# Tokenizer of a vision tower: GpSimd's first chunk products wait for VectorE's coefficients

## The reference

```
dt = exp(log_dt)
dt_Lambda = dt * Lambda                      # complex, [128 heads, 64 states]
S = exp(dt_Lambda[..., None] * t - P_max)    # t = 0..511
num = exp(dt_Lambda_neg) - 1
den = exp(dt_Lambda_neg * L) - 1
x = den * Lam
Wc = W * num * conj(x) / (x * conj(x) + 1e-7)
K = einsum('chn,hnl->chl', Wc, S).real       # [16, 128, 512]
h = concat([cls_tok, K])                     # the tokens of all later layers
```

## Time and profile before

| | |
|---|---|
| median of 3 runs | 1603.04 us (1602.81 to 1603.46) |
| the profiled execution's own time | 1603.07 us |
| its span, first to last instruction | 1601.3 us |
| TensorE busy | 1392.8 us (87%) |
| VectorE busy | 844.9 us (53%) |
| ScalarE busy | 373.8 us (23%) |
| GpSimd busy | 480.3 us (30%) |
| mean granted TensorE clock | 0.964 |

### The profile page before, as it was taken

One profiled execution on the slowest core, in us unless ns is written; L12 is line 12 of the kernel. 1 busy time (PEld: TensorE's weight loads), 2 busy tenths in 40 slices (PEclk: granted clock), 3 DMA queues, 4 the chain that ended last, 5 costly groups with the idle time before them and its releaser, 6 DMA issues.

```text
span 1601.3 us, 20910 instructions
## 1 busy us (share of the span) xinstructions
PE 1392.8 (87%) x6461; PEld 1080.7 (67%) x6462; DVE 844.9 (53%) x1711; ACT 373.8 (23%) x711; POOL 480.3 (30%) x350
## 2 busy tenths in 40 slices
PE   0295667999899999379999899999999989899996
PEld 0293325888544444136777588888888879888895
DVE  8895488655322222464667775555555533333332
ACT  1022213211111111142223312333233212122221
POOL 0480620152144443100111025523333111333442
PEclk9999788999999999789999999999999999999998
DMA  4294003301765554600000303666656578666543
GB/s 97 53 165 65 0 0 131 127 21 42 280 161 94 95 96 76 197 26 0 1 0 1 140 20 122 195 219 211 223 202 208 215 301 294 181 182 182 95 85 40
DMA packets 87386, 193.95 MB, mean 121 GB/s; under 512 B 28657, under 2 KB 32753, under 8 KB 83825
## 3 DMA queue, kind: packets, MB, share of 16 engines
q1 hardware_dynamic: 67232, 151.18, 29.2%
q0 software_dynamic: 20096, 42.02, 14.2%
HBM read 112.24 MB, written 77.87 MB: 119 GB/s over the span
## 4 chain that ended last, share of the span: by engine, by line
PE 74%; DVE 12%; DMA 9%; issue 2%; ACT 1%; POOL 0%; SPq 0%; POOLq 0%; DVEq 0%; ACTq 0%
PE ps L1505 21%; PE ps L1565 19%; PE ps L1626 9%; PE ps L2027 6%; PE ps L1652 4%; PE ps L427 4%; DMA out<-held,moe_scratch 3%; PE ps L1599 2%; DVE held L480 2%; DMA held<-xn_rows,moe_scratch 2%; DMA out<-moe_scratch 2%; PE ps L536 1%; PE ps L776 1%; PE ps L777 1%; PE ps L1640 1%
## 5 line engine op out<-in xcount | busy, mean ns | idle before, releaser
L1565 PE MATMUL ps<-moe_rounded 128*128 128x384 f32 (+2 forms) x1800 | 374.9, 350 | 0.0
L1565 PEld LDWEIGHTS ps<-moe_rounded 128*128 128x128 f32 x1800 | 326.3, 188 | 33.2
L1275 DVE SCALAR_TENSOR_TENSOR held<-ps,moe_scratch,held 128x512 f32<-128x512 f32 (+1 forms) x255 | 187.5, 748 | 180.1 <-PE ps L1505 180.0
L1505 PE MATMUL ps<-moe_expert_parts,moe_rows_parts 128*128 (+1 forms) x1320 | 260.1, 350 | 4.7 <-DVE moe_rows_parts L1283 3.1
L1505 PE MATMUL ps<-moe_rounded 128*128 128x512 f32 (+3 forms) x885 | 240.1, 391 | 7.7 <-DVE moe_rounded L1257 5.7
L1505 PEld LDWEIGHTS ps<-moe_expert_parts,moe_rows_parts 128*128 128x128 f32 (+1 forms) x1320 | 220.5, 191 | 18.2 <-issue 5.6
L1505 PEld LDWEIGHTS ps<-moe_rounded 128*128 128x128 f32 (+2 forms) x885 | 146.1, 170 | 45.9 <-DVE moe_rounded L1257 8.1
L1289 DVE TENSOR_TENSOR moe_scratch<-moe_scratch,ps 128x256 f32<-128x256 f32 (+1 forms) x80 | 37.7, 471 | 235.2 <-ACT moe_scratch L1486 235.2
L1626 PE MATMUL ps<-moe_experts,moe_scratch 128*128 x320 | 145.8, 599 | 1.7 <-ACT moe_scratch L1472 1.2
L1381 POOL TENSOR_TENSOR moe_split_parts<-moe_scratch,moe_split_parts 128x704 fp32r<-128x704 f32 (+2 forms) x48 | 88.6, 1851 | 172.9 <-ACT moe_split_parts L1461 172.8
L1365 POOL DMA_INDIRECT slot_tokens<-moe_scratch x68 | 73.5, 1081 | 170.3 <-DVE held L1275 163.6
(11 more groups left out here) (305 smaller groups left out, 1692.1 us busy)
## 6 DMA issues: line engine op xcount, KB each, us to landing
moe_expert_parts<-expert_parts SPq DMA_DIRECT2D x8, 3840.0 KB, 14.9
expert_parts<-moe_split_parts SPq DMA_DIRECT2D x32, 704.0 KB, 3.7
moe_scratch<-in_ffn_gate_up SPq DMA_DIRECT2D x32, 352.0 KB, 4.9
xn_rows<-moe_xn SPq DMA_DIRECT2D x2, 4096.0 KB, 12.8
moe_experts<-in_ffn_gate_up SPq DMA_DIRECT2D x8, 1024.0 KB, 12.5
expert_parts<-moe_split_parts SPq DMA_DIRECT2D x8, 1024.0 KB, 4.7
moe_scratch<-in_ffn_sh_gate_up SPq DMA_DIRECT2D x15, 512.0 KB, 3.5
tokens<-sb SPq DMA_DIRECT2D x16, 256.0 KB, 4.5
```

Source lines behind the costliest of these rows:

```text
L1275: v.scalar_tensor_tensor(out=hb[0:rows, t, :], in0=ps[0:rows, ADDED[t % 3], :], scalar=sg[0:rows, t:t + 1], in1=hb[0:rows, t, :], op0=ALU. ...
L1505: mm = t.matmul(out, lhs(k, x), rhs(k, y), start=(k == 0 and i == 0), stop=(k == ks - 1 and i == 2))
L1565: mm = t.matmul(unit_banks(u, m)[j], weights(k, x, j), xT[y][:, k, unit_cols(m)], start=(k == 0 and i == 0), stop=(k == KD - 1 and i == 2))
```

## The change

GpSimd waits, once, ahead of its first chunk, for the semaphore that VectorE raises to 2 at the end of the coefficients (L344). The wait for the tables of the first quarter remains. All other instructions and their order on each engine stay.

```diff
             u = k % 2
             hh = slice(k * HC, (k + 1) * HC)
             if u == 0:
+                if k == 0:
+                    g.wait_ge(tabr, 2)
                 g.wait_ge(t_in[k // 2], 12 * 16 if k else 8 * 16)
             if k >= 2:
                 g.wait_ge(prod, 2 * (k - 1))
```

## The result

The changed kernel takes 1591.27 us (median of 6 runs, 1590.54 to 1597.37), the kernel before 1603.89 us (6 runs, the three shown earlier among them, 1602.81 to 1605.84). The ratio is 0.9928 with a 95% interval of 0.9915 to 0.9942, so 0.58% to 0.85% faster. The forecast was 1592.0 us. The profiled execution took 1593.97 us, with a span of 1592.2 us.

A forecast was written before the change was run, and what follows sets the result against it. Bound: a chain ending last, three quarters TensorE, whose tokenizer start waits on VectorE coefficients stalled beside GpSimd. 1603.05 - 11.1 = 1592.0 us, other terms zero; range 1588.6 to 1595.8 us.

The forecast's parts named there:

- The stalls: VectorE's coefficients, L320 to L328: six instructions held by GpSimd's beside them; removing this gains 11.1 us, bounds 10.8 to 11.2.
- Rival A: VectorE's coefficients: only tensor-scalar instructions speed up, two-input ones stay slow; gain 3.9 us, 1599.2 us; chance 0.03.
- GpSimd's lateness: Tokenizer start: GpSimd begins at 49.0 us, chunk 0 ready at 55.4 us, 2.6 us before TensorE needs it; no cost.
- The price I named for lost cover: Tokenizer start: if chunk 0 came too late, the cost would be the excess of GpSimd's end over 58.0 us.
- Products beside L355 to L363: First factor products: VectorE's PSUM-reading instructions run beside GpSimd's late products without being slowed; cost nothing.
- The bound from above: First factor products: if L355, L362 and L363 were held like L320, TensorE would start 1.4 us later than forecast.
- What does not shift with the block: Later stages: TensorE's granted clock may cost or save one or two slow stretches, 3.5 us either way, net zero.
- rival C: Expert and attention stages: more slow clock stretches make the kernel slower, needing 14.3 us, seven more of 1.97 us; chance 0.02.

The follow-up runs named there:

- the half version: Changed kernel edited so chunk 0 is released by the tables as before and only chunk 1 waits for VectorE's coefficients; 1598.93 us, ratio 0.9964 to the kernel before.
- the run that spent the cover: Changed kernel edited so GpSimd's first product waits for ScalarE's first factor copy instead of VectorE's coefficients; 1593.66 us, ratio 0.994 to the kernel before.
- the later release: Changed kernel edited so GpSimd starts at VectorE's reciprocal, beside the wide coefficient instructions; 1603.03 us, ratio 0.9995 to the kernel before.

## Why the prediction was right

*The stalls.* They were GpSimd's doing, and they were worth what the chain of waits said. The seven instructions from L320 to L329's start now take 42.62 - 40.83 = 1.79 us by the chain, against my 1.65 us: the second of a pair costs 0.17 to 0.21 us, and the 64-column ones 0.26 and 0.28 us instead of 0.23. The gain is 12.73 - 1.79 = 10.94 us there, 11.02 us at TensorE's start. Three runs carry it as a cause: half the products give half the delay, products moved along VectorE's stream move the holds, and products set where no transfer lands make six new holds. So these two engines don't meet only at semaphores, as the opening has it: an instruction that waits for none can still be held by the other engine's.

*Rival A and the page behind it.* The two-input instructions are held as well, whatever that sentence of the page names. Another page of the Trainium skill, "GPSIMD Engine Reference", section Key points, names both kinds, two-port modes and two SBUF inputs. The traces agree with it for GpSimd's products and copies (2.01 us for L320 in the half version, 1.26 us for L297 beside copies); beside memsets the two-input instructions were not held (0.42 us).

*GpSimd's lateness.* It was ready at 55.41 us, 2.7 us ahead of L363, with 2.6 forecast. The price I named for lost cover, GpSimd's excess over 58.0 us, was too high: the run that spent the cover lost 1.5 us at TensorE's start and had 0.14 us of it left at the last chunk.

*Products beside L355 to L363.* No cost, as forecast: 2.29 and 1.22 us, and 2281 ns as the mean of L355 over the eight chunks:

```profile
L355 DVE TENSOR_TENSOR sb<-sb,ps 128x2048 f32<-128x2048 f32 x8 | 18.2, 2281 | 4.4 <-ACT ps L405 4.4
```

The bound from above of 1.4 us was too small, though nothing came to need it. It let VectorE's own work lie inside the hold, the same error as in the forecast for the later release. With both engines taking turns, as there, L355 would have started its work at 55.41 us, and L363 would have ended near 64 us and not 59.4 us: an estimate from 2.29, 1.22 and 1.95 us each, some 6 us more than without holds.

*What does not shift with the block.* I named only the clock, one or two slow stretches either way, put at a net of zero. The term is there: where the granted clocks differ, the distance goes down by 2.5 us in the attention layer and up again by 1.8 us behind its last products. The step from 11.0 to 11.8 us ahead of the first expert layer is not explained here. What I did not name is the second expert layer, where 2.0 us went in this pair and 5.0 us in another profile of the changed kernel (11.8 us ahead at the last L1565, 1278.2 us, and 6.8 us at its end, 1594.5 us). What sets that, the gathers or the token stores, was not tested and stays open.

*Luck in the number.* The gain read from medians is 12.6, 12.2 and 10.9 us in three comparisons, around the 11.0 us of the tokenizer and no more precise than that. The forecast lies within 0.8 us of the median because two differences offset each other: the kernel before stands 0.8 us higher over six runs than over the three that I started from, and the gain came out 1.5 us larger. Those three runs lay closer together (0.65 us) than this kernel's do; single executions of the kernel before reach from 1596.7 to 1608.0 us, those of the changed kernel from 1589.5 to 1597.4 us. For rival C, seven slow stretches (13.8 us) would not have reached the 14.3 us that it needed; it took eight.

## What to carry to other kernels

When several short VectorE instructions each last as long as the GpSimd instruction beside them, the two take turns: compare each with its own shape elsewhere in the trace, and the excess along the chain of waits is what moving GpSimd will give, as long as the work behind moves as a block. Put GpSimd's work where VectorE waits or reads PSUM, as long as its consumer has time; the cheapest place here was the stretch in which VectorE waited for a transfer. Before counting a late start as a loss, see whether the engine that starts late is faster than the one that paces it.

## What was not expected of the hardware

A GpSimd memset, which reads nothing, holds VectorE's fp32 tensor-scalar instructions (0.29 to 1.07 us, as long as the memset's 6.05 / 6 = 1.01 us) and not its two-input ones (0.42 us), while a copy holds both.

TensorE's granted clock is shown as 1.00 from the start until well behind the tokenizer, but the durations don't bear that out. Busy time by stretch of the kernel before, and then its transposes L536 in three windows (143 to 148, 153 to 157 and 249 to 254 us): least, median and greatest ns, first and last start.

```profile
144.00:148.00 4.00, 3.31 (x17) 2.91 (x15) 3.97 (x12) 2.93 (x5) 0.00 (x0) 1.00 0.01 2
```

```profile
L536 PE MATMUL ps<-held,sb x16: 421/421/447, 143.6 to 146.8; 128*128 128x128 f32 x16
...
L536 PE MATMUL ps<-held,sb x24: 272/273/273, 153.8 to 156.3; 128*128 128x128 f32 x24
...
L536 PE MATMUL ps<-held,moe_xn x18: 421/421/473, 250.2 to 253.8; 128*128 128x128 f32 x18
```

The third group runs where the granted clock is shown as 0.50, and has the 421 ns of the first, where it is shown as 1.00. So from 143 to 148 us the clock was most likely at 1.2 GHz and the column is wrong there; for the tokenizer itself no trace shows which it was. It takes nothing from the comparison, since both kernels have it alike (the changed kernel's transposes take 417 ns from 132.6 us and 272 ns from 141.8 us).
